# First attention of a two-layer block: all probabilities split in high and low parts, two of six low parts made by VectorE

## The reference, cut to what matters

```python
def _L0_attn_ref(hidden_states, Wq, Wk, Wv, Wo):
    H, NH = 512, 16
    HD = H // NH
    ...
    q, k, v = (proj(Wq), proj(Wk), proj(Wv))
    ...
    scores = jnp.einsum('bhqd,bhkd->bhqk', q, k) / math.sqrt(HD)
    scores = jnp.where(causal, -jnp.inf, scores)
    attn = jax.nn.softmax(scores, axis=-1)
    out = jnp.einsum('bhqk,bhkd->bhqd', attn, v)
    ...
x = x + _layernorm(_L0_attn_ref(_layernorm(x, axis=-1), L0_attn_Wq, L0_attn_Wk, L0_attn_Wv, L0_attn_Wo), axis=-1)
```

## Time and profile before

| | us |
|---|---|
| median of 3 runs | 3373.97 (3365.05 to 3374.67) |
| profiled execution | 3367.46 |
| its span | 3365.7 |
| busy in the span: PE, PEld | 2872.0 (85%), 2292.9 (68%) |
| DVE, ACT, POOL | 1936.0 (58%), 1185.6 (35%), 943.1 (28%) |
| front stage | 0 to about 208 |
| first attention | about 213 to 620 |

### The profile page before, as it was taken

One profiled execution on the slowest core, in us unless ns is written; L12 is line 12 of the kernel. 1 busy time (PEld: TensorE's weight loads), 2 busy tenths in 40 slices (PEclk: granted clock), 3 DMA queues, 4 the chain that ended last, 5 costly groups with the idle time before them and its releaser, 6 DMA issues. The chain is left out here.

```text
span 3365.7 us, 42283 instructions
## 1 busy us (share of the span) xinstructions
PE 2872.0 (85%) x14636; PEld 2292.9 (68%) x14636; DVE 1936.0 (58%) x3582; ACT 1185.6 (35%) x2287; POOL 943.1 (28%) x664
## 2 busy tenths in 40 slices
PE   7969999769999994567999999579999992688894
PEld 6846666548888883356888887468888871466773
DVE  5648888562332324355666666556666666666756
ACT  2226666321111111133444443324444441233331
POOL 1227777631111112022000000330000002277633
PEclk9969999879999997789999999799999995799997
DMA  5764443220001004740000000400000003111002
GB/s 173 232 202 128 132 126 108 70 100 19 19 20 36 0 1 149 281 158 27 22 33 22 33 22 18 153 27 23 33 22 33 22 18 137 38 38 38 0 1 100
DMA packets 123391, 236.96 MB, mean 70 GB/s; under 512 B 12832, under 2 KB 67104, under 8 KB 122496
## 3 DMA queue, kind: packets, MB, share of 16 engines
q1 hardware_dynamic: 123264, 235.32, 21.0%
HBM read 162.14 MB, written 72.88 MB: 70 GB/s over the span
## 5 line engine op out<-in xcount | busy, mean ns | idle before, releaser
L1067 POOL TENSOR_TENSOR l0a_probs_hl<-l0a_probs,l0a_probs_hl 128x896 fp32r<-128x896 f32 (+1 forms) x128 | 285.2, 2249 | 107.1 <-ACT l0a_probs L995 107.1
L1299 PE MATMUL l1a_obank<-l1a_pT_hl,l1k_v_hl 128*128 128x512 f32 (+3 forms) x1152 | 300.1, 369 | 7.1 <-DVE l1a_pT_hl L1372 7.1
L1372 DVE TENSOR_TENSOR l1a_pT_hl<-l1a_work,l1a_pT_hl 128x512 fp32r<-128x512 f32 (+3 forms) x384 | 212.9, 555 | 155.2 <-ACT l1a_pT_hl L1332 155.0
L1325 ACT ACTIVATE l1a_probs<-l1a_scores,l1a_row 128x128 f32<-128x128 f32 (+7 forms) x256 | 189.6, 742 | 317.3 <-DVE l1a_row L1362 317.3
L1279 PE MATMUL l1a_scores<-l1k_kT_hl,l1a_qa_hl 128*128 128x512 f32 (+3 forms) x1152 | 291.1, 361 | 1.5 <-ACT l1a_probs L1325 1.5
L1415 POOL TENSOR_TENSOR l1a_q_stage<-l1k_qpe,l1a_ones 128x512 fp32r<-128x512 f32 x32 | 33.4, 1043 | 872.7 <-PE l1a_work L1307 816.8
L1704 DVE TENSOR_TENSOR f0f_hid<-f0f_silu,f0f_ubank 128x512 f32<-128x512 f32 x64 | 44.0, 688 | 319.6 <-PE f0f_ubank L1639 319.6
L1332 ACT CAST l1a_pT_hl<-l1a_work 128x512 fp32r<-128x512 f32 (+3 forms) x384 | 183.7, 478 | 106.5 <-PE l1a_work L1290 105.3
L1307 PE MATMUL l1a_work<-l1a_wov,l1a_oT_hl 128*128 128x512 f32 x768 | 214.3, 401 | 5.0 <-DVE l1a_oT_hl L1391 3.0
L1759 POOL TENSOR_TENSOR f0f_h_hl<-f0f_hid,f0f_h_hl 128x512 fp32r<-128x512 f32 x64 | 82.6, 1291 | 475.8 <-ACT f0f_h_hl L1676 475.8
L1362 DVE TENSOR_REDUCE l1a_row<-l1a_scores 128x1 f32<-128x128 f32 (+7 forms) x256 | 189.6, 750 | 44.1 <-PE l1a_scores L1282 44.0
(11 more groups left out here) (258 smaller groups left out, 6230.0 us busy)
## 6 DMA issues: line engine op xcount, KB each, us to landing
v_dram<-l0f_v_rows SPq DMA_DIRECT2D x24, 768.0 KB, 4.0
qk_dram<-l0f_stage SPq DMA_DIRECT2D x128, 128.0 KB, 2.5
l1a_wov<-wov_dram SPq DMA_DIRECT2D x32, 512.0 KB, 3.5
l0a_v_stage<-v_dram SPq DMA_DIRECT2D x32, 384.0 KB, 4.3
l1a_wabs<-wabs_dram SPq DMA_DIRECT2D x32, 384.0 KB, 3.8
l0a_q_stack<-qk_dram SPq DMA_DIRECT2D x32, 256.0 KB, 3.6
l0a_k_stack<-qk_dram SPq DMA_DIRECT2D x32, 256.0 KB, 3.8
wov_dram<-w1a_wov SPq DMA_DIRECT2D x16, 512.0 KB, 3.3
```

The costliest lines, as they stand in the source:

```text
L1067: nc.gpsimd.tensor_tensor(probs_hl[:, r, 1, 0:wide], probs[:, r, 0:wide], f32(probs_hl[:, r, 0, 0:wide]), ALU.subtract).then_inc(low_done, 1)
L1299: last = pe.matmul(obank[:, c:SPAN], src["v_hl"][:, a, n, :], pT_hl[:, ring(n, s), b, c:SPAN], start=(n == 0 and i == 0), stop=(n == QT * ...
L1325: nc.scalar.activation(probs[s][:, first:first + wide, :].rearrange("p k c -> p (k c)"), scores[:, n % S_AHEAD, 0:wide * P], ACT.Exp, bias ...
L1372: nc.vector.tensor_tensor(pT_hl[:, r, 1, c:SPAN], work[:, slot, c:SPAN], f32(pT_hl[:, r, 0, c:SPAN]), ALU.subtract).then_inc(work_free[slo ...
```

## The change

Units 1 and 5 are treated like the other four. ACT takes their exponential twice (L994 runs for all six units), the low part is made by a subtraction, and PE multiplies `v_stage` by both parts. The subtraction of these two units (`LOWS_BY_DVE`) stands in DVE's list at the place L of the step; POOL keeps the other four. There are two semaphores for low parts in place of one. The values in plain fp32 disappear: `v32_rows`, its memsets, copies and stores in the front stage, `v32_dram`, and `v32_stage` with its loads. The number of steps between L and P (`LAG`, 3) is the same in both kernels.

```diff
-                    sp.wait_ge(ones_set, 7)
+                    sp.wait_ge(ones_set, 3)
...
-                if tt in KT_FP32:
-                    sp.wait_ge(v32_made, made_upto(t))
-                    sp.dma_start(v32_dram[b, :, KT_FP32.index(tt)].rearrange("g p c -> p g c"),
-                                 v32_rows[:, t % 2].rearrange("p (g j) c -> p g (j c)", g=KT)).then_inc(v32_stored[t % 2], 16)
...
-                    if t % TB in KT_FP32:
-                        wait(act, v32_stored[t % 2], 16 * ((made_upto(t) - 1) // 2))
-                        nc.scalar.copy(v32_rows[:, t % 2, :, 2 * HD0:3 * HD0], in_heads(t)).then_inc(v32_made, 1)
...
-                nc.vector.memset(v32_rows[:, slot, :, 0:HD0], 0.0).then_inc(ones_set, 1)
-                nc.vector.memset(v32_rows[:, slot, :, HD0:2 * HD0], 1.0).then_inc(ones_set, 1)
...
-IN_FP32 = (1, 5)
-KT_FP32 = [kt for kt in range(TB) if kt % QT >= 2]
+LOWS_BY_DVE = (1, 5)
...
-                if quarter == 0:
-                    sp.dma_start(v32_stage[:, slot].rearrange("p t j c -> p t (j c)"),
-                                 v32_dram[b, g].rearrange("t p c -> p t c")).then_inc(v_loaded[slot], 16)
...
-                    if u in IN_FP32:
-                        pe.wait_ge(exp_done, n + 1)
-                    else:
-                        pe.wait_ge(low_done, lows_upto(n))
+                    mine, count = lows_upto(n)
+                    pe.wait_ge(low_done[mine], count)
                     for kt, c, at, _ in parts:
-                        span = slice(at, at + SPAN - c)
-                        if u in IN_FP32:
-                            steps = [(v32_stage[:, group % 2, KT_FP32.index(kt), j, :], probs[:, r, span])]
-                        else:
-                            steps = [(v_stage[:, group % 2, kt, j, :], probs_hl[:, r, part, span]) for part in range(2)]
...
-                    if n % U not in IN_FP32:
-                        nc.scalar.activation(probs_hl[:, r, 0, 0:wide], sbank[:, n % 2, 0:wide], ACT.Exp)
+                    nc.scalar.activation(probs_hl[:, r, 0, 0:wide], sbank[:, n % 2, 0:wide], ACT.Exp)
...
+                elif kind == "L" and n % U in LOWS_BY_DVE:
+                    _, _, wide = pieces(n % U)
+                    r = n % RING0
+                    dve.wait_ge(exp_done, n + 1)
+                    nc.vector.tensor_tensor(probs_hl[:, r, 1, 0:wide], probs[:, r, 0:wide],
+                                            f32(probs_hl[:, r, 0, 0:wide]), ALU.subtract).then_inc(low_done[True], 1)
...
-                if kind == "L" and n % U not in IN_FP32:
+                if kind == "L" and n % U not in LOWS_BY_DVE:
```

More of the change, by code:

```diff
@@ L503, in front_uses, with front_layer0 @@
     return {event: n for n, event in enumerate(e for e in front_order() if e[0] in "WXQK")}
-def front_layer0(nc, m, ident, src, weights, rope, qk_dram, v_dram, v32_dram):
+def front_layer0(nc, m, ident, src, weights, rope, qk_dram, v_dram):
     XR = 4
@@ L519, in front_layer0 @@
     v_rows = m.sb("v_rows", [P, 2, NH, 3 * HD0], F32R)
-    v32_rows = m.sb("v32_rows", [P, 2, NH, 3 * HD0])
     ones = m.sb("ones", [P, 1])
@@ L537, in front_layer0 @@
     v_stored = [m.sem(f"v_stored{i}") for i in range(2)]
-    v32_made = m.sem("v32_made")
-    v32_stored = [m.sem(f"v32_stored{i}") for i in range(2)]
-    made_upto = lambda t: sum(i % TB in KT_FP32 for i in range(t + 1))
     use = front_uses()
@@ L595, in _ @@
                 sp.wait_ge(v_stored[i], 16 * NT // 2)
-                sp.wait_ge(v32_stored[i], 16 * made_upto(NT - 1) // 2)
                 sp.wait_ge(qk_stored[i], 16 * 4 * GROUP_HEADS * NT // 4)
@@ L763, in lows_upto @@
     h, u = divmod(unit, U)
-    return h * (U - len(IN_FP32)) + sum(v not in IN_FP32 for v in range(u + 1))
+    mine = u in LOWS_BY_DVE
+    per = len(LOWS_BY_DVE) if mine else U - len(LOWS_BY_DVE)
+    return mine, h * per + sum((v in LOWS_BY_DVE) == mine for v in range(u + 1))
 def steps_layer0():
@@ L794, in uses_layer0, with attention_layer0 @@
     return out
-def attention_layer0(nc, m, ident, ident_bf, mask, qk_dram, v_dram, v32_dram, sums_dram, inverse_dram, out, next_load):
+def attention_layer0(nc, m, ident, ident_bf, mask, qk_dram, v_dram, sums_dram, inverse_dram, out, next_load):
     mbank = m.ps("mbank", [P, 2, SPAN])
@@ L809, in attention_layer0 @@
     v_stage = m.sb("v_stage", [P, 2, TB, GROUP_HEADS, 3 * HD0], F32R)
-    v32_stage = m.sb("v32_stage", [P, 2, len(KT_FP32), GROUP_HEADS, 3 * HD0])
     o_rows = m.sb("o_rows", [P, 2, 2, SPAN])
@@ L825, in attention_layer0 @@
     scores_full, exp_done = m.sem("scores_full"), m.sem("exp_done")
-    low_done = m.sem("low_done")
+    low_done = {True: m.sem("low_by_dve"), False: m.sem("low_by_pool")}
     values_done = m.sem("values_done")
@@ L966, in _ @@
                     if u == 0 and j == 0:
-                        pe.wait_ge(v_loaded[group % 2], 80 * (group // 2 + 1))
+                        pe.wait_ge(v_loaded[group % 2], 64 * (group // 2 + 1))
                     if parts[0][0] == 0:
                         wait(pe, o_done, 2 * (h - 1) + s + 1)
-                    if u in IN_FP32:
-                        pe.wait_ge(exp_done, n + 1)
-                    else:
-                        pe.wait_ge(low_done, lows_upto(n))
+                    mine, count = lows_upto(n)
+                    pe.wait_ge(low_done[mine], count)
                     for kt, c, at, _ in parts:
-                        span = slice(at, at + SPAN - c)
-                        if u in IN_FP32:
-                            steps = [(v32_stage[:, group % 2, KT_FP32.index(kt), j, :], probs[:, r, span])]
-                        else:
-                            steps = [(v_stage[:, group % 2, kt, j, :], probs_hl[:, r, part, span]) for part in range(2)]
-                        for part, (values, weights) in enumerate(steps):
-                            last = pe.matmul(obank[0:3 * HD0, s, c:SPAN], values, weights, start=(kt == 0 and part == 0),
-                                             stop=(kt == QT * (s + 1) - 1 and part == len(steps) - 1))
+                        for part in range(2):
+                            last = pe.matmul(obank[0:3 * HD0, s, c:SPAN],
+                                             v_stage[:, group % 2, kt, j, :],
+                                             probs_hl[:, r, part, at:at + SPAN - c], start=(kt == 0 and part == 0),
+                                             stop=(kt == QT * (s + 1) - 1 and part == 1))
                     last.then_inc(values_done, 1)
@@ L1067, in _ @@
                     nc.gpsimd.tensor_tensor(probs_hl[:, r, 1, 0:wide], probs[:, r, 0:wide],
-                                            f32(probs_hl[:, r, 0, 0:wide]), ALU.subtract).then_inc(low_done, 1)
+                                            f32(probs_hl[:, r, 0, 0:wide]), ALU.subtract).then_inc(low_done[False], 1)
                 group, late = divmod(i - (U * (GROUP_HEADS - 1) + 8 + LAG), U * GROUP_HEADS)
@@ L2075, in two_layers @@
             v_dram = dram("v_dram", [B, KT, TB, P, 3 * D // KT])
-            v32_dram = dram("v32_dram", [B, KT, len(KT_FP32), P, 3 * D // KT])
             sums_dram, inverse_dram = dram("sums_dram", [NH * B, S]), dram("inverse_dram", [NH * B, S])
@@ L2079, in two_layers @@
                 front_layer0(nc, m, ident, x0, [view(f"L0_attn_W{n}") for n in "qkv"],
-                             tuple([a[f"{n}_{w}0"] for w in "qk"] for n in ("cos", "sin")), qk_dram, v_dram, v32_dram)
+                             tuple([a[f"{n}_{w}0"] for w in "qk"] for n in ("cos", "sin")), qk_dram, v_dram)
             with phase("l0") as keep:
@@ L2084, in two_layers @@
                 with phase("l0a") as m:
-                    attention_layer0(nc, m, ident, ident_bf, mask, qk_dram, v_dram, v32_dram, sums_dram, inverse_dram, oT,
+                    attention_layer0(nc, m, ident, ident_bf, mask, qk_dram, v_dram, sums_dram, inverse_dram, oT,
                                      (raw[:, :, :], view("L0_attn_Wo")))
```

## The result

| | before | after |
|---|---|---|
| median, us | 3373.0 (3365.1 to 3374.7) | 3525.5 (3524.9 to 3527.6) |
| ratio | | 1.046 (95%: 1.045 to 1.047) |
| span of the profiled execution | 3365.7 | 3525.8 |
| front stage, to the first L938 (L921 after) | 213.2 | 207.2 |
| attention, from there to the end of its last O | 407.4 | 572.0 |

The change costs 152.5 us. The spans differ by 160.1, and the attention stage by 164.6; the front stage gives 6.0 back. The forecast of 3422 had the sign, but its range ended at 3470.

What follows compares the result with a forecast made beforehand. It took DVE to bound steps 3 to 5 of each head, PE and DVE alternating elsewhere. Terms +60.0, -7.8, -3.0, +1.6, -0.26 gave +50.5 on 3367.46: 3418, taken as 3422 from the runs' median; range 3400 to 3470.

Steps and rivals of the forecast that it cites:

- Front stage, -3.0: Before the attention: dropped memsets free 1.9 us on DVE, two dropped stores 1.1 us on SP's queue.
- PE's short units and ACT: Attention: two-part products save PE 0.26 us a head in step 2, nothing in step 4; ACT's added exponentials cost nothing.
- DVE is the limit in steps 3 to 5: Each attention head: DVE works back to back there with 0.26 us idle, so DVE time added in step 5 is paid in full.
- Unit 5's subtraction, 2.01 us: Step 5 on DVE: it waits for POOL's unit 0 subtraction, ends 0.40 us after it, and delays L1036 by 2.01 us.
- the term for the last two heads: Last two attention heads, POOL the limit: each of four DVE subtractions holds POOL up by 0.40 us, +1.6 us.
- Unit 1's subtraction, 0: Step 1 on DVE: its 0.47 to 0.54 us fit into idle time; about 0.3 us a head if POOL were in the way.
- Step 0's work will be 2 us later against POOL's, so unit 2's subtraction on POOL is over by then.: Step 1 of a head: reason given for unit 1's subtraction on DVE not meeting POOL, cost nothing.
- The clock's rival: Attention, step 0: PE stands 1.8 us a head, its clock falls for 3.2 us; +45 us, to 3467; chance 0.2.
- the granted clock in the stage is under 0.9: Attention stage: listed as a sign that the forecast is wrong.

Runs made afterwards that it cites:

- nolock: Changed kernel with DVE's subtraction for units 1 and 5 replaced by a reduction of the same width reading one SBUF tensor: 3373.2 us, ratio 1.000.
- join_warm: Changed kernel with the maxima's halves joined by a one-input reduction, plus six and two extra PE products in step 0: 3420.5 us, ratio 1.014.
- actcopy: Kernel before, with the copy L1036 out of PSUM on ACT and DVE's addition moved behind the next step's reductions: 3364.3 us, ratio 0.997.
- join: Changed kernel with DVE's join of the maxima's halves written as a reduction with one SBUF input: 3450.0 us, ratio 1.023.
- warm: Changed kernel with extra PE products (6, 2 and 2 a head) where PE would stand in steps 0 and 1: 3465.3 us, ratio 1.028.
- mix4: Changed kernel, unit 5's subtraction one step earlier on DVE, unit 1's on POOL, maxima joined by one-input reduction, L1036 copy on ACT, addition later: 3382.1 us.

## Why the prediction was wrong, point by point

- **Front stage, -3.0.** Measured -6.0. The memsets gave 2.0: PE's first weight product starts at 32.47 and not at 34.48 (1.9 forecast). The rest is on SP, and there the term was mis-sized. Not only do the two stores vanish; the last two groups of 16 q and k stores are issued in 9.44 and 9.77 us, in place of 10.88 and 11.33. That gives 3.0 us more. The cause stays open: with the fp32 stores gone, fewer stores are under way beside them, but the group before these took 9.44 us against 9.56, hardly less.

```profile
179.24 9.44 SPq L564 DMA_DIRECT2D qk_dram<-l0f_stage  x16
...
189.20 9.77 SPq L564 DMA_DIRECT2D qk_dram<-l0f_stage  x16
```

- **PE's short units and ACT.** Right. In nolock and join_warm DVE's idle time in step 2 is 0.55 or 0.56 us in place of 0.78, so PE is 0.23 faster (0.26 forecast). ACT's exponentials cost nothing, as nolock shows.
- **DVE is the limit in steps 3 to 5.** Right for added time: nolock's 0.55 us less the 0.23 would make 12.3, and 12.3 it is. For removed time it holds for about 0.4 us only (actcopy).
- **Unit 5's subtraction, 2.01 us.** Right in size and in mechanism: 2.01 at the median of join, 1.99 to 2.02 in join_warm in all but the first and the last two heads, its end 0.41 to 0.42 us after POOL's (0.40 forecast). In the changed kernel, where the phases move, its mean is 2.24. The rule from the Trainium skill (SBUF — State Buffer, Who interferes with whom), that an instruction with two SBUF inputs and a GpSimd one that reads SBUF exclude each other, holds for the new operation, with these numbers. With the join and the clock out (join_warm) the kernel is 1.5 us from the forecast, and part of that closeness is luck: a head without the reciprocal takes 13.91 us against 13.74, some 5 us over 30 heads, while the front's extra 3 us and the term for the last two heads (1.6 forecast, 0.2 measured: 17.9 us between their last copies against 17.7) stand against that.
- **Unit 1's subtraction, 0.** Right where the phases are as forecast (0.54 us in join_warm and at the median of the changed kernel). In the changed kernel, with shifted phases, its mean is 1.03.
- **The step that failed: "Step 0's work will be 2 us later against POOL's, so unit 2's subtraction on POOL is over by then."** It looked at unit 1's subtraction alone. The work that comes 2 us later includes the join, an operation with two SBUF inputs that was already there, and it lands in the middle of unit 2's subtraction. The same part of the prediction had quoted the join as evidence for the exclusion (0.16 and 0.27 us) and then did not move it along. Its wait averages 0.8 us a head (mean 0.93, less 0.16), up to 1.7, and delays the transposition and all of step 1. It costs 44.9 us with PE kept busy and 75.5 without. With this step put right and nothing else (join) the kernel takes 3450.0 us, inside the range.
- **The clock's rival.** It named the right stop and the right length (1.8 us), but got a chance of 0.2. Its price of 45 us was no underestimate for the clock alone, which costs 29.6 (join against join_warm). Beside the join's wait it is 60.2 us, and the 3.2 us at half rate become 6 to 10 us a head. The evidence against it, one fall behind the stops of 1.7 to 1.9 us of the last feed-forward (the trace has six of them, not seven), did not carry over: between 430 and 510 us five long stops (1.82 to 2.64 us) are followed by five falls. And it left out that stage's four longer stops, of 2.01, 2.04, 3.95 and 4.07 us, each of which is followed by 1.2 GHz. The one of 2.04 us in the kernel before, and the window behind it:

```profile
2922.30 2.23 PE L1649 MATMUL f1f_ybank<-f1f_wT,f1f_h_hl 128*128 128x512 f32 x7 [2.04 <-DVE f1f_h_hl L1708]
...
2923.90:2927.20 3.30, 3.30 (x9) 2.60 (x8) 1.02 (x2) 0.00 (x0) 3.22 (x3) 0.52 0.00 0
```

  The prediction's own list of signs had "the granted clock in the stage is under 0.9"; it was 0.77.
- **The range.** It ended at the clock's rival, and the clock with the forecast's own wait lies inside it (3450.0 in join). The join's wait was in no case; both start from the same 2 us, so a case that has one tends to have the other, and together they cost 30.6 us more than one by one.

What stays open: which property of a stop decides whether the clock falls. In join, equal stops of 1.82 us before the products at 425.91 and 458.41 are followed by 1.2 GHz for 6.3 us from 428.9 and for 3.1 us from 459.3, and a longer one, of 2.33 us before 306.29, is followed by none (the granted clock is 1.00 from 306 to 320 us). So the length alone does not decide. No run varied the stop's length alone, and why the added products of warm and join_warm keep the clock up was not looked into beyond that they fill the stop (0.69 us is left of it in join_warm).

## What to carry to other kernels

When an edit shifts an engine's work in time, list every operation on it that excludes another engine, the old and tiny ones too, and lay the shifted times against that engine's. An operation of 4 elements a partition can wait for 2 us. Where such an operation can be written with one SBUF input, do it: the join as a reduction was worth 75 us in the changed kernel and 5 to 7 in the better ones. And price a new stop of PE together with the other waits that start from the same delay: here the clock alone cost 30 us, the join's wait alone 45, and both 105.

## What the runs showed of the hardware

- A DVE operation with two SBUF inputs ends a fixed time after POOL's, by its own size: 128x384 some 0.41 us later (0.412 to 0.422), 128x4 some 0.02 us (0.017 to 0.026). That holds however long before POOL's end they start (up to 2.08 us). There is one exception in the attentions of all runs: in join_warm, at 653.23 us, the subtraction takes 0.54 us, and POOL's operation, which began 0.18 us before it, takes 2.94 us in place of 2.4. So POOL was the one that was held. With one SBUF input or none nothing is held: the copies and additions above take 0.68 to 0.69 us inside POOL's operations.
- DVE does not get in between POOL operations that follow each other without a wait: 5.02 us across three of them in mix4. In the last feed-forward, where POOL's next operation came 0.08 us after the end, it did after the first.
- Reductions of DVE out of SBUF run inside POOL's operations at full speed (0.16 us for the join, 1.06 for 880 columns).
- Extra work on PE made a kernel faster: 10 products more a head, -60 us, with a granted clock of 0.98 against 0.76.
